# A block of attention and experts on eight cores: the queries' and keys' step is finished within the next one, normalization runs in three parts, and the first expert's weights are split two steps after their load

## The chip, the cores and the metric

The kernel runs on all 8 cores of one Trainium2 chip. The time is in device microseconds, of the slowest core of an execution. TensorE (PE in the rows) multiplies, VectorE (DVE) and ScalarE (ACT) do the elementwise work, GpSimd (POOL) gathers and loads, SyncE (SP) issues most transfers. Each has its own queue of instructions, in the order of the program, and they wait for each other on semaphores.

## The reference

Layer normalization, then differential attention and a mixture of experts on the same normalized rows, and a residual:

```python
xn = _layernorm(x, axis=-1)
x = x + attn(xn, Wq, Wk, Wv, Wproj, lq1, lk1, lq2, lk2) + ffn(xn, gate_w, ...)

# attn: B, T, C = 8, 2048, 1024; H = 8 heads, hd = 64
q = apply_rotary(rmsnorm((x @ Wq.T).reshape(B, T, 2 * H, hd)), cos, sin)
k = apply_rotary(rmsnorm((x @ Wk.T).reshape(B, T, 2 * H, hd)), cos, sin)
v = (x @ Wv.T).reshape(B, T, H, 2 * hd)
attn = softmax(causal(q k' / sqrt(hd)))           # of both halves of a head
out = (attn[:, :, 0] - lam * attn[:, :, 1]) @ v   # lam from lq1, lk1, lq2, lk2
out = layernorm(out) * (1.0 - LAMBDA_INIT) @ Wproj.T

# ffn: sigmoid gate, the best 2 of 8 experts; one mean weight per expert over all tokens
out = sum_e where(sel_e, mlp_e(x) * wmean_e, 0) + mlp_shared(x)
```

## The kernel before

Each core has one of the eight sequences (T = 2048 rows, 16 tiles of 128) for everything but the gate's statistics: an expert's mean weight needs all 8 x 2048 rows, so each core also reads the other seven sequences in bf16 (56 remote tiles of 256 rows). Values are kept as a bf16 high part and a bf16 low part, and a product is three matmuls (high-high, high-low, low-high).

The stage of this study is the first loop, `for s in range(96)`. s counts six chunks of 512 weight columns by 16 row tiles (t): chunks 0 and 1 are the values, 2 and 3 the keys, 4 and 5 the queries. One step is:
- `qkv_mm(s)`: 24 matmuls of 128x512 into one of three PSUM banks; it waits for what read the bank three steps earlier (`ev`).
- in chunk 0 also the normalization of a later row tile (`ln_a(t + 3)`: `ln_a1` is statistics on VectorE, `bn_stats` twice and `bn_aggr`, then logarithm and exponential on ScalarE; `ln_a2` normalizes on VectorE, tile xr, and makes the high part on ScalarE, tile xrow; `ln_a3` is the low part on VectorE), the gate's matmuls (`gate_mm`, copied to lgl) and `ln_b(t + 2)`, 16 transposes and two copies into xnT. Once, in step 4, `setup_b` computes the constants lamneg (attention) and cs8 (column sums of the gate's weights, eight matmuls).
- `v_post` for values (tile vrow), `qk_post` for keys and queries: square of the projection (ScalarE, tile sqb), its sums (VectorE, ss8), logarithm and exponential (ScalarE, ri8), rotary products and sum (VectorE, t1b and t2b), scaling by ri8 (VectorE), high part (ScalarE, qrow) and low part (VectorE). Three steps later `qk_tr` transposes, and ScalarE copies to the staging tile stag.
- from step 16 on, in ten of 13 steps, `rq_step`: GpSimd loads a remote tile, ScalarE squares the one loaded two such steps ago (tile xqs, `rq_conv`), TensorE takes the gate's sums of the one before that (`rq_mm`), VectorE copies them (st10).
- a weight step, t % 4 == 2: a quarter of the next chunk's weights is split in two parts (`w_split`, tile wb; for chunk 1 also centred, tile wmn).

After the loop come the shared expert (up and gate, `gu_step`, then down, `dn_step`, each for two halves of the rows), attention, the routed experts and the output projection. In the second down part, 16 steps, SyncE also issues twelve loads of the first routed expert's weights, and ScalarE and VectorE split them (`x0_quant`; `wpop(keep)` splits the oldest loads until keep are left). There SyncE's order in a step is: store of the last step's result (SH from xsb), load of the row piece for two steps later into the buffer that this store frees, a load for attention's first head, a load of weights (tile wld, three buffers).

Order on each engine is that of the Python code. Lines in the rows are mostly those of helpers: L221 is every `tensor_tensor`, L241 every ScalarE activation, L238 every ScalarE copy, L213 every matmul, L217 every transpose, L117 every plain transfer. So tiles tell instructions apart.

Of the kernel before, what the change touches and what calls it, by code (L numbers as in the profile page):

```python
# [16 lines left out]
C = 1024  # L17
# [136 lines left out]
def build_program():  # L154
# [178 lines left out]
    io_f = t1b[:, 0:128]  # L333
# [35 lines left out]
    xrR = ring("xr", 3)  # L369
    xsR = ring("xs", 2)  # L370
    x_free = [None] * 3
    xrow_free = [None] * 2
# [6 lines left out]
    def ln_load(t):  # L379
        ld_x[t] = xrR.go(SP, xr[t % 3][:, :], xloc[t * 128:t * 128 + 128, :], x_free[t % 3])  # L380

    ln_hl = {}

    def ln_a(t):
        ln_a1(t)
        ln_a2(t)
        ln_a3(t)
# [3 lines left out]
    def ln_a1(t):  # L391
        b, k = xr[t % 3], t % 2
        for i in range(2):
            tk = V.do(lambda e, i=i: e.bn_stats(lnst[:, k, i * 6:i * 6 + 6],
                                                b[:, i * 512:i * 512 + 512]), ld_x[t])
        tk = V.do(lambda e: e.bn_aggr(lnmv[:, k, :], lnst[:, k, :]), tk)
        s1 = act(lnr[:, k, 0:1], lnmv[:, k, 1:2], AF.Ln, tk, t_set, bias=LN_EPS)
        s1 = act(lnr[:, k, 0:1], lnr[:, k, 0:1], AF.Exp, s1, scale=-0.5)
        ln_sc[t] = (s1, tk)

    def ln_a2(t):
        b, k = xr[t % 3], t % 2
        xn = ts(V, b[:, :], b[:, :], lnmv[:, k, 0:1], lnr[:, k, 0:1],
                AL.subtract, AL.mult, *ln_sc[t])
        ln_hl[t] = scp(xrow[k][:, 0, :], b[:, :], xn, *(xrow_free[k] or ()))

    def ln_a3(t):
        b, k = xr[t % 3], t % 2
        hi = ln_hl[t]
        lo = tt(V, xrow[k][:, 1, :], b[:, :], xrow[k][:, 0, :], AL.subtract, hi)  # L410
        x_free[t % 3] = lo
        ln_hl[t] = (hi, lo)

    def ln_b(t):
        k = t % 2
# [23 lines left out]
    def setup_b():  # L439
# [115 lines left out]
    def qk_post(s, pe):  # L555
        ch, t = divmod(s, 16)
        isq = ch >= 4
        o = bk[s % 3]
        k2, k3 = s % 2, s % 4
        sq = act(sqb[:, :], o, AF.Square, pe, small.get("ss"))  # L560
        small["ss"] = vsum(ss8[:, k2, :], sqb.rearrange("p (a b) -> p a b", b=64), sq)
# [3 lines left out]
        cb = vw(coss, t * 64, [[0, 8], [1, 64]])  # L565
        o8 = o.rearrange("p (a b) -> p a b", b=64)
        t18 = t1b.rearrange("p (a b) -> p a b", b=64)
        t28 = t2b.rearrange("p (a b) -> p a b", b=64)
        x1 = tt(V, t18, o8, cb, AL.mult, pe, small.get("t1"), *cs_lds)
        tt(V, t28[:, :, 0:32], o8[:, :, 32:64], vw(sins, t * 64, [[0, 8], [1, 32]]), AL.mult)  # L570
        x2 = tt(V, t28[:, :, 32:64], o8[:, :, 0:32], vw(sins, t * 64 + 32, [[0, 8], [1, 32]]),
                AL.mult)
        ev[s] = (sq, x2)
        x3 = tt(V, t1b[:, :], t1b[:, :], t2b[:, :], AL.add, x1, x2)
        x3 = tt(V, t18, t18, vw(ri8, k2 * 8, [[1, 8], [0, 64]]), AL.mult, x3, a)
        hi = scp(qrow[k3][:, 0, :], t1b[:, :], x3, qrow_free[k3])
        lo = tt(V, qrow[k3][:, 1, :], t1b[:, :], qrow[k3][:, 0, :], AL.subtract, hi)
        small["t1"] = lo
        later.append((s + 3, lambda: qk_tr(s, k3, hi, lo)))
# [56 lines left out]

    ln_load(0)
# [258 lines left out]
    gu_free[2] = [y for x in xrow_free for y in x]  # L896
# [133 lines left out]
    for hf in range(2):  # L1030
# [40 lines left out]
        for r in range(16):  # L1071
# [705 lines left out]
```

How the kernel before makes its waits and increments, by code:

```python
    def need(self, toks):  # L44
        for tk in toks:
            if tk is None:
                continue
            h, v = tk
            if self.seen.get(id(h), 0) < v:
                self.seen[id(h)] = v
                self.waits.add(len(self.q))
                self.q.append(lambda e, h=h, v=v: e.wait_ge(h, v))
# [21 lines left out]
        def f(e):  # L74
            with e.If_eq(reg(), val):
                n = n0
                for i, fn in part:
                    if i in waits:
                        fn(e)
                    if i in incs:
                        if n:
                            e.wait_ge(self.sem, n)
                        e.sem_inc(self.sem, 1)
                        n += 1
                assert n == n1
            with e.Else():
                for _, fn in part:
                    fn(e)
# [1040 lines left out]
    def expert_split():  # L1129
        x, i, k, ld = wx_tok.pop(0)
        if i in (0, 4) and x >= 2:
            end = end_gu if i == 0 else end_dn
            G.q.append(lambda e: e.wait_ge(end, 2 ** (x - 1)))
        to = gub[x % 2][:, 2 * i:2 * i + 2] if i < 4 else dnb[x % 2][:, 2 * i - 8:2 * i - 6]
        src = wx[:, k, :].rearrange("p (a b) -> p a b", b=1024)
        a = gcp(to[:, :, 0, :], src, ld)
        b = tt(G, to[:, :, 1, :], src, to[:, :, 0, :], AL.subtract, a)
        wx_free[k] = b
        if i in (3, 5):
            sem = (rd_gu if i == 3 else rd_dn)[x]
            G.need([b])
            G.q.append(lambda e: e.sem_inc(sem, 1))
```

## Time and profile before

| | us |
|---|---|
| median of 3 runs (2833.97 to 3150.67) | 2836.65 |
| the profiled execution | 2834.62 |
| its span on the slowest core (core 6) | 2833.1 |
| spans of the 8 cores | 2804.4 to 2833.1 |
| TensorE, VectorE, ScalarE busy | 2606.8, 1356.0, 1159.5 |

A row of busy time by stretch gives the stretch, its length and for each engine the busy us in it (with the count of instructions), then TensorE's mean granted clock as a share of full speed, the share of time in which the DMA engines were busy, and GB/s. A row of the timeline is: start, duration, engine, line, operation, output<-inputs, shapes, count; in brackets how long the engine had been idle before it and whose end released it. Several equal instructions in a row are merged (x2) under one start and one duration. A row of waits names the waiting instruction, what it waited for, the total, the number and the longest.

### The profile page before, as it was taken

What the parts mean: (1) busy time and instruction counts of PE and PEld (TensorE: products, weight loads), DVE (VectorE), ACT (ScalarE), POOL (GpSimd) and SP (SyncE); (2) the same over time, 40 slices, a digit from 0 to 9 for tenths busy, and PEclk for the clock granted to TensorE, in tenths of its full rate; (3) what the DMA queues carried; (4) which work ended last, traced back from release to release, by engine and by line L of the source; (5) the groups of instructions that cost most, each with busy time, mean ns of one, the idle gap of its engine ahead of it and who ended that gap; (6) DMA issues with size and microseconds to landing.
All of it is one profiled execution on the core that took longest, in us unless ns stands there. A gap on an engine that the chain in (4) does not pass through costs nothing.

```text
span 2833.1 us, 54143 instructions; the slowest of 8 cores (2804.4 to 2833.1 us)
## 1 busy us (share of the span) xinstructions
PE 2606.8 (92%) x20236; PEld 1471.1 (52%) x20236; DVE 1356.0 (48%) x2182; ACT 1159.5 (41%) x1654; POOL 388.4 (14%) x256
## 2 busy tenths in 40 slices
PE   5799998888988999969999999999899999999889
PEld 3445444444433444426777777777444444444334
DVE  6533666566663122227888888888212221111233
ACT  3434555555322012116777777777222222224100
POOL 0000000000000000000010100000563365350111
PEclk8999999999999999989999999999999999999999
DMA  5646556553437351254433344201444444332476
GB/s 179 165 129 128 111 99 117 107 98 82 119 104 189 101 163 42 75 162 132 117 110 104 125 117 121 62 19 31 140 164 142 150 157 153 143 123 76 151 251 208
DMA packets 181185, 351.82 MB, mean 124 GB/s; under 512 B 11296, under 2 KB 105120, under 8 KB 180896
## 3 DMA queue, kind: packets, MB, share of 16 engines
q1 hardware_dynamic: 152192, 240.85, 28.2%
q0 software_dynamic: 28704, 106.97, 15.1%
q8 instruction: 200, 3.28, 0.5%
q14 instruction: 89, 0.73, 0.1%
HBM read 260.74 MB, written 116.39 MB: 133 GB/s over the span
## 4 chain that ended last, share of the span: by engine, by line
PE 62%; DVE 14%; ACT 10%; issue 7%; DMA 5%; SPq 1%; DVEq 0%; ACTq 0%; PEldq 0%; POOL 0%; POOLq 0%
PE psum L213 40%; PE psum L1483 13%; PE psum L1536 7%; DVE t1b L221 3%; DVE pl L221 3%; PE psum L217 3%; DMA SH<-xsb 2%; ACT xqs L241 2%; ACT p L241 2%; DVE oo L221 1%; ACT stag L238 1%; DVE t2b L221 1%; ACT sqb L241 1%; DVE ph L232 1%; SPq L117 1%
## 5 line engine op out<-in xcount | busy, mean ns | idle before, releaser
L213 PE MATMUL psum<-wb,xnT 128*128 128x512 bf16 x2304 | 541.3, 394 | 6.0 <-DVE wb L221 4.8
L213 PE MATMUL psum<-vt,ph 128*128 128x129 bf16 (+1 forms) x4352 | 404.7, 219 | 41.0 <-DVE pl L221 25.1
L213 PEld LDWEIGHTS psum<-vt,ph 128*128 128x128 bf16 x4352 | 342.0, 98 | 110.9 <-issue 82.3
L1483 PE MATMUL psum<-gub,xgT 128*128 128x512 bf16 x1776 | 390.6, 380 | 7.6 <-issue 7.6
L213 PE MATMUL psum<-vt,pl 128*128 128x129 bf16 x2176 | 388.6, 222 | 0.0
L213 PEld LDWEIGHTS psum<-wb,xnT 128*128 128x128 bf16 x2304 | 226.8, 101 | 280.1 <-issue 46.2
L221 DVE TENSOR_TENSOR pl<-p,ph 128x1024 bf16<-128x1024 f32 (+1 forms) x288 | 336.0, 1167 | 59.2 <-DVE ph L232 28.0
L213 PE MATMUL psum<-xnT,guw 128*128 128x512 bf16 x1536 | 337.3, 383 | 6.5 <-DVE t2b L221 3.3
L241 ACT ACTIVATE p<-psum 128x1024 f32<-128x1024 f32 (+1 forms) x288 | 280.2, 973 | 70.6 <-PE psum L213 68.3
L1483 PEld LDWEIGHTS psum<-gub,xgT 128*128 128x128 bf16 x1776 | 172.3, 98 | 210.7 <-issue 10.4
L213 PEld LDWEIGHTS psum<-xnT,guw 128*128 128x128 bf16 x1536 | 151.3, 99 | 191.0 <-issue 13.8
L213 PE MATMUL psum<-qa,ka 128*128 128x512 bf16 (+3 forms) x640 | 221.6, 349 | 3.1 <-ACT p L241 2.0
L213 PE MATMUL psum<-qz,kb 128*128 128x512 bf16 (+3 forms) x640 | 220.1, 349 | 0.0
L213 PEld LDWEIGHTS psum<-vt,pl 128*128 128x128 bf16 x2176 | 211.7, 97 | 0.0
L213 PE MATMUL psum<-dnw,hT 128*128 128x512 bf16 x768 | 176.6, 394 | 31.8 <-DVE xsb L221 21.8
L1536 PE MATMUL psum<-dnb,hTm 128*128 128x512 bf16 x888 | 199.2, 381 | 6.7 <-ACTq L83 5.7
L221 DVE TENSOR_TENSOR mh<-msl,psum 128x512 f32<-128x512 f32 x37 | 25.5, 688 | 338.5 <-ACT msl L241 338.5
L213 PE MATMUL psum<-wpb,oT 128*128 128x512 bf16 x768 | 169.5, 384 | 17.8 <-DMA oT<-OD 11.6
L238 ACT CAST ph<-p 128x512 bf16<-128x512 f32 (+1 forms) x288 | 171.8, 597 | 23.1 <-ACT p L241 1.1
L1180 POOL DMA_INDIRECT XG<-xsc,slot x32 | 41.7, 1304 | 960.5 <-ACT ph L238 559.8
L232 DVE CAST ph<-p 128x512 bf16<-128x512 f32 (+1 forms) x288 | 117.8, 409 | 59.8 <-ACT p L241 46.5
L1536 PEld LDWEIGHTS psum<-dnb,hTm 128*128 128x128 bf16 x888 | 87.0, 98 | 113.3 <-issue 10.3
(198 smaller groups left out, 2833.3 us busy)
## 6 DMA issues: line engine op xcount, KB each, us to landing
wx<-wexp POOLq DMA_DIRECT2D x42, 1024.0 KB, 5.5
xqb<-xrem POOLq DMA_DIRECT2D x56, 512.0 KB, 6.2
XG<-zer SPq DMA_DIRECT2D x39, 512.0 KB, 6.2
xgr<-XG SPq DMA_DIRECT2D x39, 512.0 KB, 5.2
YD<-yb SPq DMA_DIRECT2D x39, 512.0 KB, 3.8
wld<-wsgu SPq DMA_DIRECT2D x32, 512.0 KB, 5.6
wld<-wqkv SPq DMA_DIRECT2D x24, 512.0 KB, 6.8
xr<-xloc SPq DMA_DIRECT2D x16, 512.0 KB, 4.7
```

What stands on the lines that cost most here:

```text
L117: lane.q.append(lambda e: e.dma_start(out, in_, **kw).then_inc(sem, 16))
L213: return PE.do(lambda e: e.matmul(o, lhsT, rhs, start=start, stop=stop, skip_group_check=skip), *toks, sig=sig)
L217: return PE.do(lambda e: e.matmul(o, data, idb[:, :], is_transpose=True), *toks, sig=sig)
L221: return lane.do(lambda e: e.tensor_tensor(o, a, b, op), *toks)
L232: return V.do(lambda e: e.tensor_copy(o, a), *toks)
L238: return S.do(lambda e: e.copy(o, a), *toks)
L241: return S.do(lambda e: e.activation(o, a, func, **kw), *toks)
L1180: fr.append(sgR.fn(G, lambda e, i=i: e.indirect_dma_start(out=XG[:, :], out_offset=bass.IndirectOffsetOnAxis(ap=slot[:, i, t:t + 1], axis= ...
L1483: x = e.matmul(bk[g], xgT[k][:, hl, cci, :], gub[p][:, cci, wl, g * 512:g * 512 + 512], start=cci == 0 and hl == 0 and wl == 0, stop=cci = ...
L1536: x = e.matmul(bk[2 + co], hTm[k][:, hl, ic, :], dnb[p][:, ic, wl, co * 512:co * 512 + 512], start=ic == 0 and hl == 0 and wl == 0, stop=i ...
```

## The change

Four edits:
- `qk_post` is cut. The scaling, high and low part of step s - 1 are issued within step s: the scaling ahead of the rotary products, the high part behind the square on ScalarE, the low part ahead of the rotary sum. The sum of squares (ss8) and its logarithm and exponential come last. t1b has two buffers; the second lies where xrow was in chunk 0.
- Normalization runs in three parts for three tiles: in step t of chunk 0 the low part of tile t + 2, the normalization and high part of t + 3, the statistics of t + 4 (`ln_ahead`). xr has four buffers instead of three, xrow three instead of two (the new ones lie where qrow is later), loads are issued for t + 5.
- `setup_b`: the eight matmuls wait for the early constants (`t_set`) and no longer for lamneg.
- `x0_quant` is followed by `wpop(2)`: the split comes two steps after its load, before it was one.

```diff
+    AQ = Space(nc, "AQ", at_q, A.at)
+    xr.append(AQ.take("xr3", [128, C]))
+    xrow.append(AQ.take("xrow2", [128, 2, C], BF16))
+    t1b = [t1b, nc.alloc_sbuf_tensor_at("t1b1", [128, 512], F32, offset=at_xrow).ap()]
...
-        t_s2 = tk
         for cci in range(8):
             tk = mm(bk[6][:, 0:17], onesb[:, :], gst[:, cci, :], cci == 0, cci == 7,
-                    t_s2, gl_tok[1], sig=cci == 7)
+                    t_set, gl_tok[1], sig=cci == 7)
...
         sq = act(sqb[:, :], o, AF.Square, pe, small.get("ss"))
+        fin = half.pop(s - 1, None)
+        if fin:
+            fin[0]()
+        x1 = tt(V, t18, o8, cb, AL.mult, pe, sq, small.get(("t1", k2)), *cs_lds)
+        tt(V, t28[:, :, 0:32], o8[:, :, 32:64], vw(sins, t * 64, [[0, 8], [1, 32]]), AL.mult)
+        x2 = tt(V, t28[:, :, 32:64], o8[:, :, 0:32], vw(sins, t * 64 + 32, [[0, 8], [1, 32]]),
+                AL.mult)
+        ev[s] = (sq, x2)
+        if fin:
+            fin[1]()
+        x3 = tt(V, t1[:, :], t1[:, :], t2b[:, :], AL.add, x1, x2)
         small["ss"] = vsum(ss8[:, k2, :], sqb.rearrange("p (a b) -> p a b", b=64), sq)
         a = act(ri8[:, k2, :], ss8[:, k2, :], AF.Ln, small["ss"],
                 bias=64.0 * RMS_EPS if isq else RMS_EPS, scale=1.0 if isq else 1.0 / 64.0)
         a = act(ri8[:, k2, :], ri8[:, k2, :], AF.Exp, a, scale=-0.5)
...
+        half[s] = qk_fin(s, k2, k3, t1, x3, a)
+    def qk_fin(s, k2, k3, t1, x3, a):
+        def scale():
+            t18 = t1.rearrange("p (a b) -> p a b", b=64)
+            y = tt(V, t18, t18, vw(ri8, k2 * 8, [[1, 8], [0, 64]]), AL.mult, x3, a)
+            half[s, "hi"] = scp(qrow[k3][:, 0, :], t1[:, :], y, qrow_free[k3])
+        def rest():
+            hi = half.pop((s, "hi"))
+            lo = tt(V, qrow[k3][:, 1, :], t1[:, :], qrow[k3][:, 0, :], AL.subtract, hi)
+            small["t1", k2] = lo
+            later.append((s + 3, lambda: qk_tr(s, k3, hi, lo)))
+        return scale, rest
...
+    def ln_ahead(t):
+        if t + 2 < NT:
+            ln_a3(t + 2)
+        if t + 3 < NT:
+            ln_a2(t + 3)
+        if t + 4 < NT:
+            ln_a1(t + 4)
...
-        if ch == 0 and t + 4 < NT:
-            ln_load(t + 4)
+        if ch == 0 and t + 5 < NT and t:
+            ln_load(t + 5)
...
-        if ch == 0 and 3 < t + 3 < NT:
-            ln_a(t + 3)
+        if ch == 0 and t:
+            ln_ahead(t)
...
+    for f in half.pop(95):
+        f()
...
                 if xq_i < 12:
                     x0_quant(xq_i)
-                    wpop(1)
+                    wpop(2)
```

The lists below give the order in which instructions stand on one engine; (x2) is a count. ScalarE, one step of the keys' chunk with a remote tile, before:

```order
L241 ACTIVATE sqb<-psum 128x512
L241 ACTIVATE ri_100<-ss_98 128x8
L241 ACTIVATE ri_100<-ri_100 128x8
L238 CAST qrow_91<-t1b 128x512
L241 ACTIVATE xqs_79<-xqb_74 128x2048
L238 COPY stag_92<-psum 128x8x128
L241 ACTIVATE sqb<-psum 128x512
```

and of the change:

```order
L241 ACTIVATE sqb<-psum 128x512
L238 CAST qrow_90<-t1b 128x512
L241 ACTIVATE ri_103<-ss_101 128x8
L241 ACTIVATE ri_103<-ri_103 128x8
L241 ACTIVATE xqs_79<-xqb_74 128x2048
L238 COPY stag_95<-psum 128x8x128
L241 ACTIVATE sqb<-psum 128x512
```

The copy into qrow is now that of the step before and stands ahead of the logarithm. VectorE in the same step, from the square's first reader on, before:

```order
L244 TENSOR_REDUCE ss_98<-sqb 128x8
L221 TENSOR_TENSOR t1b<-psum,coss 128x512
L221 TENSOR_TENSOR t2b<-psum,sins 128x8x32 x2
L221 TENSOR_TENSOR t1b<-t1b,t2b 128x512
L221 TENSOR_TENSOR t1b<-t1b,ri_100 128x512
L221 TENSOR_TENSOR qrow_91<-t1b,qrow_91 128x512
```

and of the change, where t1b_94 is the second buffer:

```order
L221 TENSOR_TENSOR t1b<-t1b,ri_103 128x512
L221 TENSOR_TENSOR t1b_94<-psum,coss 128x512
L221 TENSOR_TENSOR t2b<-psum,sins 128x8x32 x2
L221 TENSOR_TENSOR qrow_90<-t1b,qrow_90 128x512
L221 TENSOR_TENSOR t1b_94<-t1b_94,t2b 128x512
L244 TENSOR_REDUCE ss_101<-sqb 128x8
```

The reduction ss went from first to last, and the scaling and the low part are those of the other buffer. VectorE in the first chunk, a plain step, before:

```order
L221 TENSOR_TENSOR vrow_69<-psum,vrow_69 128x4x128
L394 BN_STATS lnst<-xr_66 128x6 x2
L396 BN_AGGR lnmv<-lnst 128x2
L226 TENSOR_SCALAR xr_66<-xr_66,lnmv,lnr 128x1024
L221 TENSOR_TENSOR xrow_71<-xr_66,xrow_71 128x1024
L232 COPY lgl<-psum 128x8
```

and of the change:

```order
L221 TENSOR_TENSOR vrow_69<-psum,vrow_69 128x4x128
L221 TENSOR_TENSOR xrow_93<-xr_92,xrow_93 128x1024
L226 TENSOR_SCALAR xr_66<-xr_66,lnmv,lnr 128x1024
L396 BN_STATS lnst<-xr_67 128x6 x2
L398 BN_AGGR lnmv<-lnst 128x2
L232 COPY lgl<-psum 128x8
```

Low part, normalization and statistics are now of three different tiles (xr_92, xr_66, xr_67), in the reverse order.

## Rows read from the trace of the kernel before

**Rows 1.** Busy time by stretch, slowest core (window: us, PE, PEld, DVE, ACT, POOL, clock, DMA).

```profile
17.00:155.40 138.40, 109.67 (x936) 62.08 (x937) 83.79 (x130) 61.17 (x95) 2.89 (x5) 0.89 0.62 177
...
262.60:729.00 466.40, 420.54 (x3529) 220.93 (x3528) 290.12 (x603) 249.37 (x377) 22.55 (x44) 0.95 0.53 101
...
1167.60:1281.20 113.60, 91.81 (x384) 38.97 (x385) 27.62 (x30) 12.54 (x12) 0.00 (x0) 0.91 0.53 157
```

**Rows 2.** Waits of TensorE, 262.6 to 729: us in total, times, longest.

```profile
PE psum L213 <- ACT xqs L241: 40.7, 14, 4.5
```

**Rows 3.** Timeline, first chunk, a plain step: start us, us, instruction.

```profile
119.88 0.69 DVE L221 TENSOR_TENSOR vrow<-psum,vrow 128x512 bf16<-128x512 f32 x1 [1.08 <-ACT vrow L238]
...
122.47 0.20 ACT L241 ACTIVATE lnr<-lnr 128x1 f32<-128x1 f32 x1
...
122.84 0.81 DVE L226 TENSOR_SCALAR xr<-xr,lnmv,lnr 128x1024 f32<-128x1024 f32 x1 [0.77 <-ACT lnr L241]
...
124.75 1.92 ACT L238 COPY xnT<-psum 128x1024 bf16<-128x1024 bf16 x2
...
127.33 0.69 DVE L221 TENSOR_TENSOR vrow<-psum,vrow 128x512 bf16<-128x512 f32 x1 [1.08 <-ACT vrow L238]
```

**Rows 4.** Timeline, first chunk: around setup_b, and the end of a weight step.

```profile
73.43 1.28 DVE L394 BATCH_NORM_STATS2 lnst<-xr 128x6 f32<-128x512 f32 x2
...
80.81 0.36 PE L213 MATMUL psum<-gst,onesb 128*128 128x17 bf16 x8 [6.95 <-DVE lamneg L226]
...
82.69 1.28 DVE L394 BATCH_NORM_STATS2 lnst<-xr 128x6 f32<-128x512 f32 x2
...
92.87 1.22 DVE L244 TENSOR_REDUCE wmn<-wld 128x8 f32<-128x1024 f32 x1
...
132.31 1.23 DVE L221 TENSOR_TENSOR wb<-wld,wb 128x1024 bf16<-128x1024 f32 x1 [1.30 <-ACT wb L238]
...
133.45 1.28 DVE L394 BATCH_NORM_STATS2 lnst<-xr 128x6 f32<-128x512 f32 x2
```

**Rows 5.** Timeline, a queries' and keys' step: ScalarE (ACT) and VectorE (DVE).

```profile
462.11 0.60 ACT L241 ACTIVATE sqb<-psum 128x512 f32<-128x512 f32 x1
462.81 0.69 DVE L244 TENSOR_REDUCE ss<-sqb 128x8 f32<-128x512 f32 x1 [0.72 <-ACT sqb L241]
463.42 0.68 DVE L221 TENSOR_TENSOR t1b<-psum,coss 128x512 f32<-128x512 f32 x1
463.60 0.21 ACT L241 ACTIVATE ri<-ss 128x8 f32<-128x8 f32 x1 [0.88 <-DVE ss L244]
463.90 0.21 ACT L241 ACTIVATE ri<-ri 128x8 f32<-128x8 f32 x1
464.02 0.75 DVE L221 TENSOR_TENSOR t2b<-psum,sins 128x256 f32<-128x256 f32 x2
464.87 0.69 DVE L221 TENSOR_TENSOR t1b<-t1b,t2b 128x512 f32<-128x512 f32 x1
...
465.73 0.69 DVE L221 TENSOR_TENSOR t1b<-t1b,ri 128x512 f32<-128x512 f32 x1 [0.17 <-DVE t1b L221]
466.51 0.62 ACT L238 CAST qrow<-t1b 128x512 bf16<-128x512 f32 x1 [2.41 <-DVE t1b L221]
467.04 1.90 ACT L241 ACTIVATE xqs<-xqb 128x2048 bf16<-128x2048 bf16 x1
...
469.74 0.60 ACT L241 ACTIVATE sqb<-psum 128x512 f32<-128x512 f32 x1
```

**Rows 6.** Instructions of the tile sqb: durations min/median/max, first and last start.

```profile
L241 ACT ACTIVATE sqb<-psum x64: 576/599/602, 262.6 to 726.2; 128x512 f32<-128x512 f32 x64
```

**Rows 7.** Timeline, TensorE, first two groups of the shared expert.

```profile
720.30 5.34 PE L213 MATMUL psum<-xnT,guw 128*128 128x512 bf16 x24
728.98 7.03 PE L213 MATMUL psum<-xnT,guw 128*128 128x512 bf16 x24 [3.34 <-DVE t2b L221]
```

**Rows 8.** Waits of SyncE's DMA queue, 1165 to 1281: us in total, times, longest.

```profile
SPq L52 <- DMA SH<-xsb: 79.4, 13, 13.5
```

More of the change, by code:

```diff
@@ L331, in build_program @@
     ri8 = A.take("ri8", [128, 2, 8])
-    io_f = t1b[:, 0:128]
+    io_f = t1b[0][:, 0:128]
     io_p = t2b[:, 0:128]
@@ L365, in cs_load @@
         cs_lds.extend(cR.all())
[L369 to L372, printed above, removed]
+    xrR = ring("xr", 4)
+    xsR = ring("xs", 3)
+    x_free = [None] * 4
+    xrow_free = [None] * 3
     xT_tok = [None] * NT
@@ L379, in ln_load @@
     def ln_load(t):
-        ld_x[t] = xrR.go(SP, xr[t % 3][:, :], xloc[t * 128:t * 128 + 128, :], x_free[t % 3])
+        ld_x[t] = xrR.go(SP, xr[t % 4][:, :], xloc[t * 128:t * 128 + 128, :], x_free[t % 4])
     ln_hl = {}
[L384 to L387, printed above, removed]
     ln_sc = {}
     def ln_a1(t):
-        b, k = xr[t % 3], t % 2
+        b, k = xr[t % 4], t % 2
         for i in range(2):
@@ L401, in ln_a2 @@
     def ln_a2(t):
-        b, k = xr[t % 3], t % 2
+        b, k, kr = xr[t % 4], t % 2, t % 3
         xn = ts(V, b[:, :], b[:, :], lnmv[:, k, 0:1], lnr[:, k, 0:1],
                 AL.subtract, AL.mult, *ln_sc[t])
-        ln_hl[t] = scp(xrow[k][:, 0, :], b[:, :], xn, *(xrow_free[k] or ()))
+        ln_hl[t] = scp(xrow[kr][:, 0, :], b[:, :], xn, *(xrow_free[kr] or ()))
     def ln_a3(t):
-        b, k = xr[t % 3], t % 2
+        b, k = xr[t % 4], t % 3
         hi = ln_hl[t]
         lo = tt(V, xrow[k][:, 1, :], b[:, :], xrow[k][:, 0, :], AL.subtract, hi)
-        x_free[t % 3] = lo
+        x_free[t % 4] = lo
         ln_hl[t] = (hi, lo)
     def ln_b(t):
-        k = t % 2
+        k = t % 3
         hi, lo = ln_hl[t]
@@ L560, in qk_post @@
         sq = act(sqb[:, :], o, AF.Square, pe, small.get("ss"))
+        cb = vw(coss, t * 64, [[0, 8], [1, 64]])
+        o8 = o.rearrange("p (a b) -> p a b", b=64)
+        t1 = t1b[k2]
+        t18 = t1.rearrange("p (a b) -> p a b", b=64)
+        t28 = t2b.rearrange("p (a b) -> p a b", b=64)
+        fin = half.pop(s - 1, None)
[9 more added lines that the diff above has]
+        x3 = tt(V, t1[:, :], t1[:, :], t2b[:, :], AL.add, x1, x2)
         small["ss"] = vsum(ss8[:, k2, :], sqb.rearrange("p (a b) -> p a b", b=64), sq)
@@ L564, in qk_post @@
         a = act(ri8[:, k2, :], ri8[:, k2, :], AF.Exp, a, scale=-0.5)
[L565 to L579, printed above, removed]
+        half[s] = qk_fin(s, k2, k3, t1, x3, a)
+    half = {}
+    def qk_fin(s, k2, k3, t1, x3, a):
+        def scale():
+            t18 = t1.rearrange("p (a b) -> p a b", b=64)
+            y = tt(V, t18, t18, vw(ri8, k2 * 8, [[1, 8], [0, 64]]), AL.mult, x3, a)
[6 more added lines that the diff above has]
+        return scale, rest
     def qk_tr(s, k3, hi, lo):
@@ L663, in build_program @@
     w0_lo(3)
-    ln_a(2)
+    ln_a1(2)
+    ln_load(4)
+    ln_a2(2)
+    ln_a1(3)
     gate_mm(0)
@@ L679, in build_program @@
                 rq_step()
+        if s == 32:
+            V.need([y for x in xrow_free for y in x])
+            S.need([x_free[3], *xrow_free[2]])
         if s == 84:
@@ L691, in build_program @@
                 ln_b(1)
-                ln_a(3)
+                ln_ahead(0)
+                ln_load(5)
                 cs_load()
@@ L895, in build_program @@
     hh_free = [ev[95], ev[95]]
-    gu_free[2] = [y for x in xrow_free for y in x]
+    gu_free[2] = [y for x in xrow_free for y in x] + [small["t1", 1]]
     def gu_step(hf, ic, bl, n):
```

1 line of the change is left out of this document (added).

## The prediction

> **What bounds the kernel now.** I read the busy time by stretch first, then the waits of TensorE, then the timeline of one step in each stretch with idle time that the change touches. In the stretch of queries' and keys' steps, 262.6 to 729 us, TensorE is idle for 466.4 - 420.54 = 45.9 us, and its mean clock of 0.95 says that about a tenth of the time runs at the lower level [rows 1]; nearly all the idle time is a wait for ScalarE's square of the remote rows [rows 2]. So neither TensorE nor the rate of ScalarE (249 of 466 us busy) sets the pace there. What does is a ring of hand-overs between ScalarE and VectorE. ScalarE squares the projection at 462.11, waits for VectorE's sum to take logarithm and exponential (463.60, 463.90), waits again for VectorE's scaling to make the bf16 copy (466.51), and only then comes to the remote rows' square (467.04), the staging copy and the next step's square at 469.74 [rows 5]. One round is 7.63 us with a remote square; without one it is 7.63 less that square's slot. All 64 rounds lie between 262.6 and 726.2 us [rows 6].
>
> In the first chunk (17 to 155.4 us) TensorE is idle for 138.4 - 109.7 = 28.7 us at a mean clock of 0.89 [rows 1]. The ring there is VectorE's low part of the values, statistics, ScalarE's logarithm and exponential, VectorE's normalization, ScalarE's bf16 copy, two copies of the transposed rows and the values' copy: 119.88 to 127.33, 7.45 us a step [rows 3]. TensorE follows it.
>
> **The change, term 1: the queries' and keys' step.** In the new order ScalarE copies the previous step's rows right after the square, and waits once instead of twice; but the sum that it waits for now stands last on VectorE, behind two rotary products, the previous step's low part and the rotary sum. What counts is the time from the square to the remote rows' square, since all that follows it is unchanged. Before: 467.04 - 462.11 = 4.93. After, by the distances of the same rows [rows 5]:
> square to the first VectorE instruction, 462.81 - 462.11 = 0.70;
> first product to second, as between 463.42 and 464.02, 0.60;
> the second product pair lasts 0.75 and its follower needs no result of it; such followers start 0.08 to 0.09 before the end (0.69 long, 0.61 apart from 462.81 to 463.42), so 0.66;
> low part to rotary sum, and rotary sum to reduction, 0.61 each;
> reduction to logarithm, 463.60 - 462.81 = 0.79; logarithm to exponential 0.30;
> exponential to the next instruction, 0.21 less the same overlap of 0.09 (ScalarE's copy is 0.62 long and its follower 0.53 behind), so 0.12.
> Sum 4.39, hence 0.54 us less per step, 7.09 instead of 7.63. The scaling for the step before needs the exponential, is ready by about 5.3 after the square, and the next square comes at 7.09 (about 5.3 without a remote square, and the copy that wants it half a microsecond later): hidden, narrowly in the few steps without remote rows. The second rotary buffer is what lets the next product start without the delayed low part.
>
> How many steps count? By the code a remote tile starts in ten of 13 steps from step 16 on, and the 56th and last is squared in step 90, so the last five of the 64 steps have no remote square; a round of about 5.3 would there be under TensorE's own step (24 matmuls alone are 5.34 [rows 7]). In the first two TensorE, and not the ring, is the later one. That leaves 57 steps, with a remote square or without, 57 x 0.54 = 30.8 us. TensorE has room: 420.5 busy less the 23 us that the low clock costs (a tenth of 466 at half rate) is about 397, so the stage could shrink by 69 before TensorE bounds it.
>
> Term 2 is the tail of that stage. TensorE's second group in the shared expert waits 3.34 us for the last rotary product and then runs at the low clock, 7.03 instead of 5.34 [rows 7]. The product now ends about 2.05 after its square (0.70 + 0.60 + 0.75), where it ended 2.66 after it, and ScalarE gains on TensorE in the last five steps. Both the wait and the slow group should go: 3.34 + 1.69 = 5.0 us.
>
> **Term 3: the first chunk.** Plain steps: the three parts now belong to three different tiles, so the piece from exponential to the transposed rows' copy, 124.75 - 122.47 = 2.28 [rows 3], leaves the ring. In come the low part ahead of the normalization (1.14, as a low part to its follower, 132.31 to 133.45 [rows 4]), the normalization ahead of the statistics (0.81 - 0.08 = 0.73) and exponential to next, 0.12 less its overlap: 1.99 in all. The ring becomes 7.16, 0.29 less. TensorE's own work at the full clock is about (109.7 - 0.11 x 138.4) / 14 steps = 6.7 us [rows 1], close under it, and after each weight step TensorE is late from its slow groups; so of nine plain steps I count three, 0.9 us. Setup_b: the eight small matmuls waited 6.95 us for lamneg, then TensorE ran slow. On VectorE the statistics at 73.43 and 82.69 are 9.26 apart instead of 7.45, and the next weight reduction comes 10.18 later (92.87), where a plain step and the reduction's 0.18 later place make 7.63 [rows 4]: 1.81 + 2.55 = 4.4 lost. Now they need only the early constants; VectorE's own small instructions for setup_b then lie in its slack before the values' copy, up to the exponential that ScalarE puts ahead of that copy, 0.5. Gain 3.9. Weight steps: VectorE still does centring, split and low part in one piece, 6.12 us from 127.33 to 133.45 [rows 3, 4], against 0.61 in a plain step; this is in the ring before and after. I count nothing. Together 4.8 us; from 2 (half of setup_b) to 9 (all nine steps and no loss of setup_b).
>
> One thing is shortened that I cost at nothing: a low part used to be made a step before its transposes, now in the same step. By my count TensorE gets to those transposes about 8.3 us after the previous low part started (1.4 to that part's end, then its own 6.7), the ring offers the new one at 7.16 + 1.4 = 8.6, so it waits some 0.3 us there. If TensorE were the later one, the same transposes would hold ScalarE up; 0.3 us a step, 3 us in all, is that case's price. SyncE's loads and stores go in the new order behind waits that are over earlier; four row buffers give each load a whole step more.
>
> **Term 4: first expert two steps ahead.** VectorE's additions no longer queue behind a split whose weights have just landed. TensorE's idle time there is 113.6 - 91.8 = 21.8 us [rows 1]. But SyncE waits 79.4 us, in 13 waits, for stores of the shared expert's output to land [rows 8], because the next row load reuses that buffer and stands ahead of the next weight load. Its issuing takes most of the rest of the 113.6. So the additions move earlier within a round whose length stays. At the end the two last splits are emptied together ahead of the same addition as before. Nothing; the upper bound is 21.8 and the low clock's part (0.91: 10 us), 32.
>
> Sum: 30.8 + 5.0 + 4.8 + 0 = 40.6. The profiled execution took 2834.6 (span 2833.1), the median is 2836.65, 2.0 above. Forecast: span 2792.5, median 2796.
>
> **A rule against it.** The independent followers on VectorE stand 0.60 to 0.61 apart at 0.69 long, the one that waits for its predecessor 0.86 (464.87 to 465.73) [rows 5]; my term 1 takes the first distance four times. The Trainium skill, VectorE: DVE Perf Modes, "The DRAIN you can't avoid", says that waits between such instructions cost nothing extra and each occupies the engine until its pipe is empty. The rows differ from it by 0.25 us between the two kinds of follower. [...]
>
> **Rivals.**
> No overlap: each of the new places takes its full duration. Then the path is 0.70 + 0.68 + 0.75 + 0.69 + 0.69 + 0.79 + 0.30 + 0.21 = 4.81, gain 0.12 x 57 = 7, in all 17: 2820. For it: VectorE now crosses between buffers and waits on two engines. Against: the rows' 0.61. The quoted section is the reason why I give it more than its rows do.
> Slower: each of the new followers pays the 0.86 of a waiting one. The path is 0.70 + 0.86 + 0.85 + 0.86 + 0.86 + 0.79 + 0.30 + 0.12 = 5.34, 0.41 more than 4.93, +23.4 over 57 steps; with terms 2 and 3 the kernel is at 2836.65 + 23.4 - 9.8 = 2850. It turns slower than before from a path of 5.10, that is from 0.18 more on each of four distances. For it: the rotary sum does wait for a VectorE result. Against: that result is two instructions old.
> The expert's part works: if SyncE's waits are not what paces that stage but the additions are, up to 32 us more go, 2764. From 16 us on it is over 2%. For it: TensorE's stalls there end in additions. Against: SyncE's waits [rows 8].
> First chunk only: if something else holds the queries' ring (VectorE's statistics copies for the remote rows, say) and term 1 is under a third of its size, the time is 2812 to 2832.
>
> **How the numbers follow.** Forecast 0.66, its own range 2786 to 2808 (path 4.39 +-0.15 gives 9 either way, the first chunk -3 to +4). No overlap 0.12. Term 1 held otherwise 0.08. Slower 0.05, nearly all of it within 2%. Expert's part 0.09. Range: from 2780 to 2820, which leaves out most of the expert's case and the slower one. About 2% is what a measurement of this kernel can tell from no change, 2780 to 2893: faster 0.10, same 0.88, slower 0.02.
>
> **What would show it.** Squares 7.09 apart in rounds with a remote square and the last at about 689 us; in them the logarithm about 4.0 after the square; the shared expert's second group at 5.3 us with no wait; no wait for lamneg; first-chunk copies of transposed rows 7.16 apart in plain steps; stretch of the shared expert's second down part still near 113 us with SyncE's waits for stores near 79. I am wrong if that last stretch is under 100 us, or if the round is under 6.9 or above 7.4.

## The result and the profile after

The changed kernel takes 0.9847 of the time of the kernel before, with a 95% interval of 0.9823 to 0.9871: on the median of the kernel before that is 2793 us, where 2796 was forecast (0.9857). The profiled execution took 2790.07 us, its span on the slowest core (core 6) is 2788.5 us. Two of the four executions behind each plain median were disturbed (neighbouring cores at a lower granted clock, the time up to 11% longer), which puts these medians at 2851.96 us for the changed kernel, above the forecast range of 2780 to 2820, and at 2920.73 us for the kernel before; the ratio comes from the other executions, and the prediction's last step, 2.0 us from span to median, has no term for such ones.

| us | before | after |
|---|---|---|
| profiled execution, span of core 6 | 2833.1 | 2788.5 |
| executions behind the ratios, span of a core, mean | 2820.2 | 2779.7 |
| first square of the queries' and keys' step, mean of 8 cores | 263.6 | 259.8 |
| first to last of these 64 squares, mean of 8 cores | 463.4 | 430.6 |
| first to last of the 16 additions of the second down part, mean | 103.1 | 104.1 |

(The second row is from four executions of the changed kernel and from six of the kernel before in the first comparison below; all other entries are of the two profiled executions.)

Busy time by stretch of the changed kernel, core 6; columns as in [rows 1]. The stretches are the first chunk, the queries' and keys' steps, and the shared expert's second down part:

```profile
17.00:155.40 138.40, 113.28 (x941) 63.48 (x942) 82.62 (x132) 62.84 (x97) 2.89 (x5) 0.89 0.73 181
256.00:692.00 436.00, 409.40 (x3549) 217.69 (x3546) 275.19 (x601) 243.37 (x375) 23.09 (x45) 0.98 0.53 111
1127.00:1241.00 114.00, 91.28 (x393) 39.25 (x392) 29.63 (x32) 13.15 (x13) 0.00 (x0) 0.91 0.52 157
```

In the middle stretch TensorE's idle time fell from 45.9 to 26.6 us and its granted clock rose from 0.95 to 0.98. The third stretch looks as before.

Instructions of the tile sqb in the same trace:

```profile
L241 ACT ACTIVATE sqb<-psum x64: 577/599/604, 261.5 to 692.0; 128x512 f32<-128x512 f32 x64
```

TensorE's waits from 256 to 692 us:

```profile
PE psum L213 <- ACT xqs L241: 22.2, 15, 2.7
PE psum L217 <- DVE qrow L221: 4.5, 8, 1.8
```

Against [rows 6] the 64 squares take 430.5 instead of 463.6 us; against [rows 2] the wait for the remote rows' square is 22.2 instead of 40.7 us.

The round itself, timeline of VectorE and ScalarE in the changed kernel (the first lines, to 438.11, are one step; the last three are one whole round, 13 us later):

```profile
433.87 0.60 ACT L241 ACTIVATE sqb<-psum 128x512 f32<-128x512 f32 x1
434.36 0.62 ACT L238 CAST qrow<-t1b 128x512 bf16<-128x512 f32 x1
434.57 0.69 DVE L221 TENSOR_TENSOR t1b<-psum,coss 128x512 f32<-128x512 f32 x1 [2.50 <-ACT sqb L241]
435.18 0.74 DVE L221 TENSOR_TENSOR t2b<-psum,sins 128x256 f32<-128x256 f32 x2
435.84 0.68 DVE L221 TENSOR_TENSOR qrow<-t1b,qrow 128x512 bf16<-128x512 f32 x1
436.44 0.68 DVE L221 TENSOR_TENSOR t1b<-t1b,t2b 128x512 f32<-128x512 f32 x1
437.04 0.68 DVE L244 TENSOR_REDUCE ss<-sqb 128x8 f32<-128x512 f32 x1
437.81 0.21 ACT L241 ACTIVATE ri<-ss 128x8 f32<-128x8 f32 x1 [2.84 <-DVE ss L244]
438.11 0.21 ACT L241 ACTIVATE ri<-ri 128x8 f32<-128x8 f32 x1
...
447.15 0.60 ACT L241 ACTIVATE sqb<-psum 128x512 f32<-128x512 f32 x1
...
451.51 1.89 ACT L241 ACTIVATE xqs<-xqb 128x2048 bf16<-128x2048 bf16 x1
...
454.20 0.60 ACT L241 ACTIVATE sqb<-psum 128x512 f32<-128x512 f32 x1
```

From the square at 433.87 to each of the others: products at 0.70 and 1.31, low part 1.97, rotary sum 2.57, reduction 3.17, logarithm 3.94, exponential 4.24, and the remote rows' square 4.36 behind its square (451.51 - 447.15). The forecast path was 4.39. The round is 7.05 (447.15 to 454.20); 7.09 was forecast, 7.63 it was before [rows 5].

Not every round is like this one. Where VectorE also splits a quarter of the weights, the scaling of the step before stands behind that split (the start of step 42, same core):

```profile
328.14 1.23 DVE L221 TENSOR_TENSOR wb<-wld,wb 128x1024 bf16<-128x1024 f32 x1 [1.71 <-ACT wb L238]
...
328.78 0.60 ACT L241 ACTIVATE sqb<-psum 128x512 f32<-128x512 f32 x1
...
329.29 0.68 DVE L221 TENSOR_TENSOR t1b<-t1b,ri 128x512 f32<-128x512 f32 x1
...
329.89 0.68 DVE L221 TENSOR_TENSOR t1b<-psum,coss 128x512 f32<-128x512 f32 x1
```

The first product comes 1.11 us after the square here, not 0.70.

TensorE's timeline at the change from that stage to the shared expert:

```profile
689.76 10.52 PE L213 MATMUL psum<-xnT,guw 128*128 128x512 bf16 x48
```

SyncE's waits from 1130 to 1242 us:

```profile
SPq L52 <- DMA SH<-xsb: 72.3, 13, 13.7
```

The shared expert's first two groups run without a break at 5.26 us each, instead of 5.34 and, behind a wait, 7.03 [rows 7]. SyncE still waits 72.3 us in 13 waits for the stores [rows 8]; before it was 79.4.

### The profile page after: what moved, and what is told of

It reads as the page before. It is cut to its first block, busy times and chain, and to the rows that moved or that the text cites. A ratio compares the mean times of both kernels' runs of the same rounds, so it can differ in the third digit from the quotient of the medians.

```text
span 2788.5 us, 53902 instructions; the slowest of 8 cores (2767.9 to 2788.5 us)
## 1 busy us (share of the span) xinstructions
PE 2589.9 (93%) x20236; PEld 1464.5 (53%) x20236; DVE 1339.2 (48%) x2182; ACT 1152.3 (41%) x1654; POOL 387.4 (14%) x256
## 4 chain that ended last, share of the span: by engine, by line
PE 63%; DVE 15%; ACT 9%; issue 8%; DMA 5%; SPq 0%; DVEq 0%; PEldq 0%; ACTq 0%; POOL 0%; POOLq 0%
PE psum L213 40%; PE psum L1519 13%; PE psum L1572 7%; DVE pl L221 3%; PE psum L217 3%; DVE t1b L221 2%; ACT p L241 2%; DMA SH<-xsb 2%; DVE oo L221 2%; ACT stag L238 1%; DMA oT<-OD 1%; DVE ss L244 1%; DVE t2b L221 1%; ACT xqs L241 1%; ACT sqb L241 1%
## 5 line engine op out<-in xcount | busy, mean ns | idle before, releaser
L213 PE MATMUL psum<-wb,xnT 128*128 128x512 bf16 x2304 | 529.7, 388 | 5.0 <-DVE wb L221 5.0
L213 PE MATMUL psum<-vt,ph 128*128 128x129 bf16 (+1 forms) x4352 | 402.9, 219 | 41.1 <-DVE pl L221 25.2
```

What stands on the lines that cost most here:

```text
L213: return PE.do(lambda e: e.matmul(o, lhsT, rhs, start=start, stop=stop, skip_group_check=skip), *toks, sig=sig)
```

## The experiments

Nine runs were made; `e_best_b` is the kernel of `e_best` again and `e_after_b` the changed kernel again, both on another chip. Every ratio is to the kernel before, run on the same chip, with a 95% interval where there is one. "First square" is the start of the first of the 64 squares of the queries' and keys' step, by which the first chunk and the rest of the values' steps are read; "the 64 squares" is the time from the first to the last.

**One part alone: `e_qk_only`.** The kernel before with the cut of `qk_post`, the second t1b and nothing else.

```diff
+    t1b = [t1b, nc.alloc_sbuf_tensor_at("t1b1", [128, 512], F32, offset=at_xrow).ap()]
...
+        half[s] = qk_fin(s, k2, k3, t1, x3, a)
...
+    for f in half.pop(95):
+        f()
```

> The kernel before with the queries' and keys' edit alone (two product buffers, last product, lower half and sum finished within the next step); first chunk and expert stage as before. Theory: the change's gain is this edit's; sqb spacing without the xqs wait falls from 5.88 to about 5.25, the 64 steps of the stage take about 430.5 instead of 463.6 us, the slow first group of the shared expert goes, and the end moves by 33 to 36 us (ratio to before about 0.9875). Rival: part of the 36 us by which TensorE's next block came earlier is from the first chunk or the expert stage; then this kernel gains under 25 us (ratio above 0.991).

Of four executions two took 3009 and 3105 us; the other two, 2789.6 and 2803.9 us, are too few for an interval; against 2833.6 they are 0.984 and 0.990. The trace is clearer:

```profile
L241 ACT ACTIVATE sqb<-psum x64: 575/598/604, 264.8 to 695.3; 128x512 f32<-128x512 f32 x64
```

The 64 squares take 430.5 us, to the tenth what the whole change gives and what was expected. First square 263.8 on the mean of the cores (before 263.6). Mean span of a core in these two 2782.6, 37.5 less than before, where the whole change has 2779.7 in the comparison above and, without the expert's part, 2782.2 in this one (`e_wpop1`). So the cut of `qk_post` is nearly all of the change, and the rest of it is worth 0 to 3 us.

**The expert's part undone: `e_wpop1`.**

```diff
-                    wpop(2)
+                    wpop(1)
```

> The changed kernel, but the routed experts' weights loaded one step ahead instead of two (the expert part of the change undone). Theory: that part is worth nothing, because SyncE's load waits for the store of the step before to land in either case; ratio as the changed kernel's 0.985, within 3 us of it. Rival: the longer lead does shorten the expert's stretch; then this kernel is 4 to 9 us slower than the changed one (ratio 0.986 to 0.988) and the stretch between the last group of experts and attention is longer by that.

Ratio 0.9863 (0.9844 to 0.9882). The 16 additions of the second down part take 101.8 us on the mean of the cores, against 104.1 with `wpop(2)` (103.9 to 105.3 in the other kernels that have it and the old row loads), 103.1 before and 103.2 in `e_qk_only`. The rival wanted 4 to 9 us more here. The two steps of lead gain nothing; if anything they lose 1 to 2 us.

**What paces that part: `e_load_late`.** The buffer that the next load needs is, one step later, one whose store has long landed.

```diff
-            if r + 2 < 16:
-                dn_load(hf * 16 + r + 2)
+            if hf == 0 and r + 2 < 16:
+                dn_load(hf * 16 + r + 2)
+            if hf == 1 and r >= 1 and r + 1 < 16:
+                dn_load(hf * 16 + r + 1)
```

> The changed kernel, but in the second half of the shared expert's down part (16 rows, 109 to 114 us) the row of the residual is loaded one step ahead, issued behind the store of its step, not two steps ahead. Theory: SyncE's loop is store, its landing, row load into the buffer that it freed; each turn waits some 7 us for the landing, which is what holds the stretch at 6.8 us a row, and with a load that needs no fresh landing the stretch falls to 88 to 95 us: 15 to 25 us less than the changed kernel (ratio 0.976 to 0.979). Rival: the landing is slow because the DMA engines are loaded, and the load itself now comes late: the stretch stays at about 110 us (ratio about 0.985) or grows.

Ratio 0.9771 (0.9753 to 0.9789); the additions take 80.1 us on the mean of the cores instead of 104.1, a gain at the upper end of the 15 to 25 us expected and a stretch under the expected 88 to 95. Busy time by stretch from the first to the last addition on core 6:

```profile
1135.70:1215.00 79.30, 77.83 (x361) 35.13 (x360) 24.01 (x28) 12.54 (x12) 0.00 (x0) 1.00 0.73 218
```

SyncE's waits in it:

```profile
SPq L52 <- DVE xsb L221: 40.7, 13, 9.2
SPq L52 <- DMA SH<-xsb: 15.4, 5, 9.0
```

The same stretch of the changed kernel:

```profile
1139.20:1242.00 102.80, 82.59 (x362) 35.82 (x361) 24.66 (x27) 12.54 (x12) 0.00 (x0) 0.92 0.55 166
```

SyncE's waits for landing stores fall from 72.3 to 15.4 us, and the others, for the addition, cost nothing, since TensorE is now busy for 77.8 of 79.3 us at the full clock. The DMA engines move 218 GB/s instead of 166, so they were not the limit. That SyncE's loop of store, landing and reuse of the buffer held this stage is shown; it is also why the additions and splits that the change moved could give nothing.

**What is left in the ring: `e_sum_first`.** The changed kernel with one line moved up.

```diff
+        small["ss"] = vsum(ss8[:, k2, :], sqb.rearrange("p (a b) -> p a b", b=64), sq)
         x1 = tt(V, t18, o8, cb, AL.mult, pe, sq, small.get(("t1", k2)), *cs_lds)
...
         x3 = tt(V, t1[:, :], t1[:, :], t2b[:, :], AL.add, x1, x2)
-        small["ss"] = vsum(ss8[:, k2, :], sqb.rearrange("p (a b) -> p a b", b=64), sq)
```

> The changed kernel with VectorE's sum of the squares moved from the end of the step's chain to its beginning, ahead of the first rotary product; the same instructions. Theory: the ring of the step (square, casts, products, sum, Ln and Exp, next square) is what sets the 6.75 us of a step, since the sum sits 3.2 us behind the square only by its place; with it first, the path square to remote square falls from 4.35 to about 1.9 us, the ring is shorter than TensorE's mean work in a step (406 of 433 us over 64 steps, 6.3 each), and the stretch of the 64 steps goes from 433 to 402 to 410 us: ratio 0.973 to 0.977. Rival: the rotary products, now 0.9 us later each, or ScalarE's copies hold the step; then the stretch shrinks by less than 10 us (ratio above 0.981).

Ratio 0.9720 (0.9697 to 0.9743), 36 us under the changed kernel. Timeline, one step:

```profile
434.16 0.60 ACT L241 ACTIVATE sqb<-psum 128x512 f32<-128x512 f32 x1
434.86 0.69 DVE L244 TENSOR_REDUCE ss<-sqb 128x8 f32<-128x512 f32 x1 [2.24 <-ACT sqb L241]
...
435.64 0.21 ACT L241 ACTIVATE ri<-ss 128x8 f32<-128x8 f32 x1 [0.38 <-DVE ss L244]
435.95 0.21 ACT L241 ACTIVATE ri<-ri 128x8 f32<-128x8 f32 x1
436.06 1.89 ACT L241 ACTIVATE xqs<-xqb 128x2048 bf16<-128x2048 bf16 x1
```

The remote rows' square comes 1.90 behind the square, as expected. The stretch of the 64 squares:

```profile
259.70:652.10 392.40, 392.40 (x3510) 213.30 (x3509) 271.39 (x597) 247.10 (x373) 22.44 (x44) 1.00 0.59 120
```

392.4 us (402 to 410 was expected): TensorE is never idle and its clock stays at 1.00, the upper of its two levels (2.4 GHz). The expectation's 6.3 us a step for TensorE was too high because it was read at a clock of 0.98 (403.9 busy us in the changed kernel's 430.5); the part at the lower level is gone too. The ring is not the limit any more: ScalarE now waits for TensorE's transposes before its staging copy (109.4 us in 60 waits). Since the sum stood first in the kernel before as well, the two edits need each other: the cut takes ScalarE's second wait, the one for the scaling, out of the ring, but puts the sum at the end of the first (463.4 to 430.6), and with the sum first the ring falls under TensorE's own work (392.4).

**Where the first chunk's gain went: `e_vd_first`.** SyncE issues the store of the values of step t - 1 ahead of the store of the normalized row of t + 2.

```diff
+            now = [f for f in later if f[0] <= s]
+            later[:] = [f for f in later if f[0] > s]
+            for _, f in now:
+                f()
             if t + 2 < NT:
                 ln_b(t + 2)
```

> The changed kernel, but in the first chunk SyncE issues the store of the values of step t-1 ahead of the store of the normalized row of t+2, as data are ready (the same instructions and bytes). In every kernel with the new order of normalization ScalarE's cast into the value row waits 2.0 to 5.0 us for that store to land, once on each core, at about 142 us; the kernel with the old order shows 0 to 1.4. Theory: it is this store's late issue that took back most of the first chunk's gain; the wait goes, and the first square of the queries' and keys' step, which comes at 261.7 on the mean of the cores, comes 2 to 4 us earlier (257.5 to 259.5); ratio 0.984. Rival: the store is slow because the five row loads of the next chunk fill the DMA engines at that moment; then the wait stays over 1.5 us and the first square stays at 261 to 262.

The wait for the store is gone on all eight cores. First square 258.1 on cores 0, 1, 4 and 5, in the middle of the expected 257.5 to 259.5. That is 3.3 to 3.6 us earlier than in the three kernels of the first comparison with the change's order of normalization (261.4, 261.6, 261.7) and 1.7 earlier than in the changed kernel's own profiled execution (259.8). Ratio 0.9844 (0.9751 to 0.9937), an interval too wide to show 3 us. How this works is read from the changed kernel on core 6, timeline of GpSimd, VectorE, SyncE, TensorE and ScalarE:

```profile
119.89 2.89 POOL L117 DMA_DIRECT2D xqb<-xrem  x5 [118.29 <-ACT vrow L238]
119.91 0.69 DVE L221 TENSOR_TENSOR vrow<-psum,vrow 128x512 bf16<-128x512 f32 x1 [3.01 <-ACT vrow L238]
...
126.03 1.22 DVE L221 TENSOR_TENSOR xrow<-xr,xrow 128x1024 bf16<-128x1024 f32 x1
...
127.37 0.32 SPq L117 DMA_DIRECT2D XN<-xrow  x1
127.84 0.54 SPq L117 DMA_DIRECT2D VD<-vrow  x1
...
137.38 5.34 PE L213 MATMUL psum<-wb,xnT 128*128 128x512 bf16 x24
142.30 0.59 ACT L238 CAST vrow<-psum 128x512 bf16<-128x512 f32 x1 [3.02 <-DMA VD<-vrow]
...
145.13 1.18 PE L217 MATMUL psum<-idb,xrow 128*128 128x128 bf16 x16 [1.82 <-DVE xrow L221]
...
146.10 6.94 PE L213 MATMUL psum<-wb,xnT 128*128 128x512 bf16 x24
...
154.38 5.34 PE L213 MATMUL psum<-wb,xnT 128*128 128x512 bf16 x24
```

the first and the last of the same three groups of 24 matmuls in the kernel before (core 6):

```profile
141.05 6.35 PE L213 MATMUL psum<-wb,xnT 128*128 128x512 bf16 x24
...
155.42 5.34 PE L213 MATMUL psum<-wb,xnT 128*128 128x512 bf16 x24
```

and `e_vd_first` (core 0):

```profile
120.34 0.69 DVE L221 TENSOR_TENSOR vrow<-psum,vrow 128x512 bf16<-128x512 f32 x1 [3.00 <-ACT vrow L238]
121.16 0.32 SPq L117 DMA_DIRECT2D VD<-vrow  x1
...
127.81 0.32 SPq L117 DMA_DIRECT2D XN<-xrow  x1
...
139.60 0.60 ACT L238 CAST vrow<-psum 128x512 bf16<-128x512 f32 x1
```

This is a weight step. The tile vrow has two buffers, so the cast at 142.30 waits for the store of two steps earlier, the one issued at 127.84. Its values are ready at 120.60, but in SyncE's queue it stands behind the row store, whose low part now comes behind the weight split on VectorE (126.03); so it is issued 7.2 us after its data, and takes 14.4 us to land (13.3 to 14.4 on the eight cores). In `e_vd_first` it is issued 0.1 us after its data and takes 6.8 us (6.7 to 9.8 on the eight cores). In the kernel before, the row store also stood first in each step, but its data were ready first, and the values' store was issued 0.1 us after its data there too (128.15 for 128.02). On TensorE the changed kernel leads the kernel before by 3.7 us at the group in front of the wait (137.38 for 141.05) and by 1.0 two groups later (154.38 for 155.42).

Transfers of the values' store from 17 to 155 us, from issue to landing, the changed kernel and `e_vd_first`, both on core 0:

```profile
DMA to landing us min/median/max: 3.7/5.5/14.0
```

```profile
DMA to landing us min/median/max: 2.0/2.1/9.4
```

In plain steps the values are ready 1.1 us before the row, and the store behind the row store takes more than twice as long to land. The 38 readings of single cores in the five profiles with the change's order of issue and of setup (cores 4 and 5 of `e_after_b`, whose first square comes after 279 us, left out) show the same from another side: on the eight cores that waited 2.3 us or less for the store the first square came at 257.9 to 259.7, on the nine that waited 3.3 us or more at 261.9 to 266.3.

**The setup's part undone: `e_lamneg`.**

```diff
+        t_s2 = tk
         for cci in range(8):
             tk = mm(bk[6][:, 0:17], onesb[:, :], gst[:, cci, :], cci == 0, cci == 7,
-                    t_set, gl_tok[1], sig=cci == 7)
+                    t_s2, gl_tok[1], sig=cci == 7)
```

> The changed kernel with the eight matmuls of the gates' bias again waiting for VectorE's negation of the weight column (the part of the change to the setup undone). Theory: that wait stood on TensorE's path before and was worth 3.9 us by the trace of before; it comes back as a wait of 3 to 7 us at about 75 us and the first square comes 3 to 4.5 us later than in the changed kernel, ratio 0.9865. Rival: the ring of the value step catches it up again and the first square stays within 1 us of 261.7.

Timeline of TensorE, core 6, `e_lamneg`:

```profile
78.63 0.37 PE L213 MATMUL psum<-gst,onesb 128*128 128x17 bf16 x8 [2.79 <-DVE lamneg L226]
79.23 6.25 PE L213 MATMUL psum<-wb,xnT 128*128 128x512 bf16 x23 [0.23 <-issue]
85.31 0.75 PE L213 MATMUL psum<-gst,xnT 128*128 128x8 bf16 x24
```

and the changed kernel:

```profile
75.56 0.35 PE L213 MATMUL psum<-gst,onesb 128*128 128x17 bf16 x8
75.77 5.34 PE L213 MATMUL psum<-wb,xnT 128*128 128x512 bf16 x24
80.94 0.75 PE L213 MATMUL psum<-gst,xnT 128*128 128x8 bf16 x24
```

The wait is 2.79 us, not 6.95 as before the change and just under the 3 to 7 expected, but the group behind it then runs slow, and the next gate matmuls are 4.4 us late. First square 264.7 (mean of cores 2, 3, 6 and 7, which lie between 263.0 and 267.7), 3.0 to 3.3 us later than the 261.4 to 261.7 of three other kernels and 4.9 later than the changed kernel's own 259.8. It could not be timed to a ratio. The theory stands: the wait is on TensorE's path, and 3 us or more hang on it; the four readings do not give its size more closely.

**All three edits: `e_best` and `e_best_b`, with `e_after_b`.** `e_best` is the changed kernel with the edits of `e_sum_first`, `e_load_late` and `e_vd_first`; `e_best_b` is the same kernel on another chip, where the changed kernel (`e_after_b`) ran too.

> The changed kernel with three edits: sum of squares first, row load of the second down part one step ahead, store of the values first. Theory: the three lie in stretches that follow each other on TensorE and share nothing, so their gains add: 39.5 (0.985 to 0.972 is 37 us), 22 and 2 to 4 us, and the time is 2733 +- 6 us, ratio 0.9635 (0.961 to 0.966). Rival: a part is given back in the stretch behind it (the routed experts' weights come no earlier); then at least 10 us are missing (ratio above 0.967).

> The kernel with the three edits together (sum first, row load one step ahead, values' store first), once more on another chip, since on the first one the executions of the kernel before were spread over 40 us and the ratio's interval (0.952 to 0.971) could not tell whether the gains add. Theory: they add; 37 + 22 to 25 + 3 us under the changed kernel, 2728 to 2736, ratio 0.9635 (0.961 to 0.966). Rival: part of it is given back behind, 10 us or more missing, ratio above 0.967.

> The changed kernel itself on the same chip, as the measure for the three edits and for the spread of the first square over cores and executions: ratio 0.985 within 0.002, values' store waited for 2 to 4 us on each core, first square at 259 to 263 on the mean of the cores. If the wait for the store is of a particular execution and not of the order of issue, it is absent on some cores here.

Ratios 0.9613 (0.9522 to 0.9705) and 0.9629 (0.9519 to 0.9740): faster than both kernels. The intervals are too wide for the question whether the gains add; the spans of single cores, in the same executions, answer it. In the second comparison a core's mean span is 2833.5 before (four executions), 2797.4 in the changed kernel (two) and 2732.9 with the three edits (four): 64.5 us less than the changed kernel, for 36 + 22 + 3 of the parts (22 is the difference of the ratios of `e_load_late` and the changed kernel; its stretch alone lost 24). Ratio of these means 0.9645, forecast 0.9635. The stretches add as well: first square 257.8, the 64 squares 392.5, the additions 79.9 us on the mean of the cores of `e_best`. The times themselves were 2744 to 2772 us, not the expected 2728 to 2736, on chips where the kernel before ran at 2841 to 2881 and not at 2834. In `e_after_b` the ratio of the mean spans is 0.9873 (0.985 within 0.002 was expected); the wait for the values' store is there on seven of eight cores, 1.6 to 3.6 us, and absent on core 5, where the store took 12.6 us.

## Why the prediction was right, and where it was not

**The step that failed** is one costed at nothing, in term 3: "SyncE's loads and stores go in the new order behind waits that are over earlier". In a weight step the wait in front of the values' store is over 7 us after its own data are ready; ScalarE then waits for this store, and of the 3.7 us by which TensorE led the kernel before on core 6, 1.0 is left.

**Term 1, the queries' and keys' step: the path right, the count near for other reasons.** The path was worked out from distances of instructions in the trace of before, and each came out within 0.02 us: 0.61 and 0.60 for followers, 0.66 behind the product pair, 0.77 to the logarithm, 0.11 behind the exponential; 4.35 to 4.36 in all for 4.39. A round is 0.58 us shorter, for 0.54. The first 59 rounds on core 6 lost 30.9 us for the 30.8 forecast, but not as 57 equal rounds: 42 of them lost 0.52 to 0.58, eleven less than 0.4 and six more than 0.6. The last four, counted as nothing here, lost another 2.2. One cost had no term: the scaling of the step before was called hidden, narrowly in the steps without remote rows. In most steps it is; but in six that begin with a weight split (42, 46, 50, 86, 88 and 90) it starts 0.50 to 0.84 us after the square, and the first product comes 1.10 to 1.44 us after it, which is 2.8 us in all. The section of the Trainium skill that was weighed against the path (VectorE: DVE Perf Modes, "The DRAIN you can't avoid") says that the next instruction does not start until the pipe is empty, and by that the path would have been 4.81; the trace does not agree, for followers in the same buffer or in another. The same section adds that a next instruction that is not held starts earlier, which the prediction left out.

**Term 2, the tail: right.** Wait and slow group are gone. TensorE's first group of the shared expert starts 30.5 us earlier (689.76 for 720.30), the next block after the first two groups 35.7 us earlier (703.29 for 739.01): 5.2 us, 5.0 forecast. Of the 30.5 us 1.0 was there already when the first chunk ended, so term 1 gave TensorE 29.5 for 30.8.

**Term 3, the first chunk: the ring right, the gain mostly lost.** On core 6 it gave 1.0 of 4.8 us; over the cores and kernels with the new order the first square came at 259.8 to 261.7, 1.9 to 3.8 before the 263.6 of the kernel before. The two parts named in the sum are there: the wait for lamneg is worth 3 us or more (`e_lamneg`; 3.9 forecast), the plain ring is 7.12 (7.16 forecast). What failed is SyncE's order. The row store's low part was now made in the same step, after the values' low part and, in a weight step, after the split, so the values' store stood ready behind a row store that was not. On all eight cores ScalarE's cast two steps later waited 2.0 to 3.0 us for it (1.6 to 5.0 in the other kernels with this order, and not at all on one core), and TensorE's next group took 6.94 instead of 5.34 us. `e_vd_first` gives this back: with it the first chunk gains 5.5 (263.6 to 258.1), the 4.8 of the forecast and a little more. How much of the slow landing is due to GpSimd's five row loads of the next stage, issued 8 us ahead of this store, is not shown: the DMA engines are busy from 128 to 142 us in all three kernels (shares of 0.99 to 1.04), and no kernel was run without these loads.

**Term 4, the first expert: right, for the reason given.** 0 forecast; the additions' stretch is 104.1 for 103.1 us. `e_wpop1` leaves it at 101.8, and `e_load_late`, which touches SyncE's loop alone, takes 24 us out of it. The bound of 32 us for this stage was of the right size too, but it belonged to SyncE's loads, not to the change.

**The rivals.** No overlap (2820), slower (2850), first chunk only (2812 and more) and the expert's part (2764) are all outside the interval of the ratio (2786 to 2800 on the median of before). Of the lines by which the forecast was to be judged, one missed: the last square came at 692.0 where about 689 was named. The terms themselves give 690.6 (726.2 less 4.8 and 30.8), and the rest is the first chunk's missing 3.7 us less the 2.3 by which the squares lost more than term 1. That the total came so near, 43 us by the ratio for 40.6, is in part luck: on core 6, where the terms were read, the span fell by 44.6 us, of which 35.7 up to the tail are the terms' doing; 5.7 more are the additions' stretch, which had been longer on this core (108.5 us) than on the others of the kernel before (100.3 to 103.9), and the other 3.2 lie elsewhere.

**What stays open.** The mean span of a core fell by 41.1 us in the profiled executions, of which first square (3.9), squares (32.8), the way from the last square to the down part (0.7) and the additions (-1.0) make 36.4. The other 4.7 us lie behind the last addition: from there to the end a core takes 1541.3 us before, 1536.6 after, and 1537.5 to 1540.5 in `e_qk_only`, `e_wpop1`, `e_sum_first` and `e_load_late`, which have the same code there, so most of it is the spread from execution to execution. It covers what the first chunk failed to give.

## What to carry to other kernels

When a ring between two engines sets the pace, add it up from the distances between starts of neighbouring rows, not from their durations, and then ask of each instruction in it whether its place is needed: the change took the scaling and the copy that waits for it out of the ring and put an instruction that heads the chain at its end, and moving that one line up was worth nearly as much again as the whole change (36 us after 43). Where edits move work between steps, write down each DMA queue's order as well, with the time at which the data of each entry are ready, in the heaviest step too: a store that is ready may stand behind one that is not. A buffer that is reloaded right behind its own store makes the store's landing part of every turn of the loop; load it one turn later, or with one buffer more.

## What the runs showed of the hardware

- VectorE's followers that write another buffer, mix bf16 and f32 outputs, or need a result that is two instructions old start 0.60 to 0.61 us behind a predecessor of 0.68 to 0.69 us, the same as plain ones.
- With TensorE never idle over 392 us its granted clock is 1.00; with 26.6 us of idle time in 436 it is 0.98 and with 45.9 in 466 it is 0.95. Taking the last 26.6 us of idle time away made the 64 squares 38.1 us shorter (430.5 to 392.4).
- The same store of values (128x1024 bf16) took 5.5 us (median of the first chunk, core 0) from issue to landing when issued 0.5 us behind the row store of its queue, and 2.1 us when issued 1.1 us ahead of it; on core 1 5.5 and 2.7. In the second chunk, which has no row stores, the two kernels do not differ so (5.3 and 5.0, on core 1 4.2 and 4.3).
